# GpSimd makes the reciprocal roots of a supergroup ahead of its row numbers

## What is computed

```python
# attention: adj is (4096, 4096)
Wh = layernorm(x) @ W_w + W_b
e = leaky_relu((Wh @ a1)[:, None] + (Wh @ a2)[None, :], 0.2)
x = x + softmax(where(adj > 0, e, NEG), axis=1) @ Wh
# mixture of experts on the layernorm of the new x
z = layernorm(x)
score = z @ Wg.T + bg
top, which = top_k(score, 2); share = softmax(top)
x = x + sum over the two of share * (relu(z @ W1[e].T + b1[e]) @ W2[e].T + b2[e])
```

## Times and profile before

| | |
|---|---|
| time, median of 3 runs | 423.79 us (420.24 to 423.88) |
| span of the profiled execution | 449.1 us |
| mean granted TensorE clock in it | 0.967 of full |
| PE busy | 395.9 us, 88% |
| DVE busy | 296.4 us, 66% |
| ACT busy | 264.4 us, 59% |
| POOL busy | 202.6 us, 45% |
| POOL L770 (power) | 3 times, 5.3 us in all |
| PE L1567, the attention product | 576 matmuls, 238.9 us |

### The profile page before, as it was taken

One profiled execution on the slowest core, in us unless ns is written; L12 is line 12 of the kernel. 1 busy time (PEld: TensorE's weight loads), 2 busy tenths in 40 slices (PEclk: granted clock), 3 DMA queues, 4 the chain that ended last, 5 costly groups with the idle time before them and its releaser, 6 DMA issues.

```text
span 449.1 us, 8413 instructions
## 1 busy us (share of the span) xinstructions
PE 395.9 (88%) x2434; PEld 262.5 (58%) x2434; DVE 296.4 (66%) x816; ACT 264.4 (59%) x451; POOL 202.6 (45%) x247
## 2 busy tenths in 40 slices
PE   2699999999999999979999999897779869899970
PEld 1355555354444444434665777686669859888960
DVE  5889879988999797999877931788105731111163
ACT  1688888377687667923679544374246425555530
POOL 3473421000416742065531777756665554455460
PEclk9799999999999999998999999999989989999995
DMA  6999998879699997975869763754655545565794
GB/s 213 362 413 351 325 318 296 357 272 377 248 329 316 343 402 266 314 283 164 306 202 375 245 192 117 215 197 160 210 193 178 186 161 179 192 210 184 238 347 139
DMA packets 45612, 116.46 MB, mean 259 GB/s; under 512 B 7517, under 2 KB 19682, under 8 KB 38902
## 3 DMA queue, kind: packets, MB, share of 16 engines
q1 hardware_dynamic: 37494, 100.81, 62.9%
q0 software_dynamic: 4320, 8.47, 5.7%
q10 hardware_dynamic: 3744, 6.56, 4.9%
HBM read 84.57 MB, written 13.07 MB: 217 GB/s over the span
## 4 chain that ended last, share of the span: by engine, by line
PE 65%; issue 9%; ACT 7%; DMA 6%; DVE 4%; another core or an unknown queue 4%; SPq 3%; POOL 1%; ACTq 0%; POOLq 0%; DVEq 0%
PE acc L1567 36%; PE acc L1669 11%; ACT G_all L1334 3%; PE hps L1653 3%; PE hps L1651 3%; PE hps L1652 3%; DMA adj<-adjT 3%; DVE prob L953 2%; PE yt L1669 2%; PE yt L1612 1%; PE pj L1528 1%; DMA xbuf<-xr,slot 1%; DMA ybuf<-wst,dest 1%; SPq L546 1%
## 5 line engine op out<-in xcount | busy, mean ns | idle before, releaser
L1567 PE MATMUL acc<-prob,Wh 128*128 128x512 f32 (+1 forms) x576 | 238.9, 556 | 7.3 <-DVE Wh L892 3.6
L953 DVE SCALAR_TENSOR_TENSOR prob<-s_bc,E_col,G_all 128x1024 f32<-128x1024 f32 (+2 forms) x160 | 170.6, 1095 | 31.9 <-PE acc L1567 19.8
L1567 PEld LDWEIGHTS acc<-prob,Wh 128*128 128x128 f32 x576 | 104.8, 192 | 103.7 <-issue 89.7
L1334 ACT ACTIVATE G_all<-adj 128x2048 bf16<-128x2048 int32 (+1 forms) x67 | 118.9, 1800 | 20.0 <-DVE prob L953 10.8
L804 POOL DMA_INDIRECT ybuf<-wst,dest x71 | 73.1, 1030 | 72.1 <-ACT wst L1417 48.2
L788 POOL DMA_INDIRECT xbuf<-xr,slot x64 | 71.5, 1117 | 57.7 <-DVE slot L1110 19.6
L1669 PE MATMUL acc<-wall,prob 128*128 x368 | 52.7, 286 | 5.5 <-issue 5.5
L1669 PEld LDWEIGHTS acc<-wall,prob 128*128 128x128 f32 x368 | 45.9, 194 | 6.6 <-issue 5.9
L1407 ACT ACTIVATE prob<-hps 128x512 f32<-128x512 f32 x46 | 27.9, 607 | 32.4 <-PE hps L1653 16.6
L1205 DVE COPY share<-slab 128x1 f32<-128x1 f32 x45 | 7.0, 155 | 58.8 <-DMA slab<-xbuf 39.4
L1407 ACT ACTIVATE wst<-hps 128x512 f32<-128x512 f32 x25 | 14.9, 597 | 26.0 <-remote 17.5
(11 more groups left out here) (245 smaller groups left out, 551.6 us busy)
## 6 DMA issues: line engine op xcount, KB each, us to landing
adj<-adjT SPq DMA_DIRECT2D x52, 1024.0 KB
adj<-adjT SPq DMA_DIRECT2D x16, 768.0 KB
s_bc<-wall SPq DMA_DIRECT2D x47, 256.0 KB
wlb<-wall SPq DMA_DIRECT2D x24, 256.0 KB
slab<-xbuf SPq DMA_DIRECT2D x71, 65.0 KB
adj<-ybuf SPq DMA_DIRECT2D x6, 512.0 KB
xs<-x SPq DMA_DIRECT2D x8, 256.0 KB, 10.4
wst<-wcat ACTq DMA_DIRECT2D x8, 256.0 KB, 4.1
```

Source lines behind the costliest of these rows:

```text
L953: nc.vector.scalar_tensor_tensor(prob[n % PR][:, 0:w], c_bc[:, P * AT[g]:P * AT[g] + w], E_col[:, u:u + 1], G[m % GR][:, k * w:(k + 1) * w ...
L1334: nc.scalar.activation(G[m % GR][:, 0:w], adj_sb[m % AR][:, 0:w], ACT.Relu).then_inc(s_G, 1)
L1567: last = nc.tensor.matmul(bank[:, 0:k * P], Wh[:, u, :], prob[n % PR][:, b * P:(b + k) * P], start=(u == 0), stop=(u == TILES - 1), skip_g ...
```

## The change

In the queue of GpSimd, `row_index(g)` moves for g = 0, 1 and 2 from part 7 to part 10, and is written behind `pow_rows(g)`, which stays at part 8. Supergroups 3 and 4 keep their order. All other engines have the same instructions in the same order.

```diff
                     for g, p in parts_of(n):
                         if p == 0 and g == 0:
                             row_ends()
-                        if p == (7 if calm(g) else 9):
-                            row_index(g)
                         if calm(g) and p == 8:
                             pow_rows(g)
+                        if p == (10 if calm(g) else 9):
+                            row_index(g)
                         if not calm(g) and (p == 5 or p == 6):
                             pow_half(g, p - 5)
```

## The result

| | before | changed |
|---|---|---|
| median of 22 runs each, in turn on one chip | 423.0 us (418.8 to 426.7) | 419.8 us (415.7 to 421.9) |
| ratio, 95% interval | | 0.9947 (0.9922 to 0.9972) |
| span of the profiled execution | 449.1 us | 419.2 us |

What follows compares the result with a forecast made beforehand. PE was taken to bound the kernel (busy 395.9 of 449.1 us). A 1.12 us shorter stop plus 1.58 us of half clock avoided gave 2.7 us, from 423.8 to 421.1 us, range 419.0 to 424.8.

Steps and rivals of the forecast that it cites:

- The path: Supergroup 1: GpSimd's wait on supergroup 0's last scatter leads through power, ACT and DVE to PE's 2.55 us stop at 201.57.
- first term: Supergroup 1: power starts 1.12 us earlier (0.9 to 1.4), passed on in full, shrinking PE's stop from 2.55 to 1.43 us.
- Supergroups 0 and 2 bring nothing: GpSimd at supergroups 0 and 2: the power waits for DVE's variance, not for scatters, so nothing is gained.
- Second term: Behind PE's stop near 200 us: the shorter stop keeps the clock up, saving 1.58 us lost at half clock.
- The sum: Whole kernel: 1.12 + 1.58 = 2.7 us less, 421.1 us, 0.6% faster; chance 0.45.
- No effect: Rival for supergroup 1: scatters may land before the variance, or ACT waits for its `adj` chunk; 423.8 us, chance 0.15.
- the rival of the stop alone: PE's stop near 200 us: clock falls anyway, leaving only the 1.1 us term; 422.7 us, chance 0.20.
- The masks and the ring: Supergroup 1: ACT's `adj` chunk is there; `prob` ring place frees at 174.53, before DVE's 174.96, so DVE gains 1.12 us.
- The slower rival: First slab stays at 228.19, PE stops there 2.7 us and the clock falls; 425.4 us, chance 0.07.
- The rival of more than the sum: Two later clock falls, at 334 and 365, up to 1.7 us each, both vanish; 417.7 us, chance 0.13.

Runs made afterwards that it cites:

- supergroups 0 and 2 alone: Against the kernel before, row numbers moved behind the power for supergroups 0 and 2 only, supergroup 1 in old order; ratio 1.0028, median 423.2 us.
- late tables alone: Kernel before, GpSimd order unchanged, with supergroup 1's table parts 16 and 17 on DVE moved from steps 21 and 22 to 24 and 27; ratio 0.9936, median 420.8 us.
- the kernel before with a second power: Kernel before with the power of supergroup 1 done twice on GpSimd; ratio 1.0003 (0.9944 to 1.0062).

## Why the prediction was right, step by step

- *The path.* Right. The wait of the row numbers on the landing, through power, product, ACT's rows, ACT's masks and DVE to PE, was the whole of the first term: the delay put back by other means brings the old stop back, and earlier scatters under the old order take away as much of it as the change does.
- *Supergroups 0 and 2 bring nothing.* Right in the traces: the power waits for the variance there in both kernels.
- *First term, 1.12 us.* The product came 1.42 us earlier with respect to the variance, 1.13 from the start of the power and 0.29 from its shorter duration, the upper end that I had kept. PE's stop came to 1.39 us where I had written 1.43, and PE went on 1.40 us earlier; the difference to 2.55 - 1.39 = 1.16 is a small delay at the rank product, 0.24 us, that had no row of its own. The term was still too small for the kernel's usual course. In the five profiles with the old order and the old scatters the row numbers started 0.97, 1.28, 1.60, 1.72 and 1.97 us behind the variance, 1.5 on average, and the profile that I had was the lowest of them. The prediction took one execution's wait for the kernel's.
- *Second term, 1.58 us for the clock.* Right for stops of 1.4 us, and right in its price: 1.5 to 1.7 us by the first slab. Wrong as a fixed sum: the fall happened behind three of five stops of 2.5 to 2.6 us. As an estimate its mean is 0.6 x 1.58 = 1.0 us. This is the term that was mis-sized upward, and it offset the first.
- *The sum.* In those five profiles the power started 1.75 us behind the variance on average (1.21, 1.53, 1.85, 1.96, 2.21), and 0.08 us in the change: 1.7 us. With 1.0 for the clock that is 2.7 us; measured 2.2 us (1.2 to 3.3). The first slab says the same: in the three profiles of kernels whose supergroup 1 is that of before (before twice, supergroups 0 and 2 alone) it came 2.96, 3.19 and 1.87 us later than in the change, 2.7 on average. No effect lies well outside the measured interval, and the rival of the stop alone, 1.1 us, just below it. But the same rival with the wait at its mean, 1.7 us, lies inside: the times alone don't show the second term; what speaks for it are the profiles and the granted clock of the runs. So the forecast of 2.7 us held, with one term too small and the other too large; that the two errors cancelled is luck.
- *The masks and the ring.* Right: ACT's `adj` chunk was there, and DVE was not held by the ring; it waited 0.56 us for the masks, where the working gave 174.96 - 174.53 = 0.43.
- *The slower rival, the first slab.* It didn't happen in the change. The kernel with late tables alone stopped there for 0.93 us, so the place is as close as feared.
- *The rival of more than the sum.* The falls at 334 and 365 of the first profile are absent from the second profile of the kernel before as well. They were no part of the kernel's usual course, and 417.7 us had no ground in them.

## What to carry to other kernels

A wait in an in-order queue holds up whatever stands behind it, so put what others wait for ahead of what only you need, and compare when each becomes ready. Follow the delay along the chain to the engine that bounds the kernel: where that chain has no slack, one microsecond there is one microsecond in the end, though it may show as stops at several places, or as slow work that hides a part of them. And take more than one profile before sizing a term: here the wait ranged from 1.0 to 2.0 us from execution to execution, and the clock behind a stop came out either way.

## What the runs showed of the hardware

- A stop of PE of 2.5 to 2.6 us, with the granted clock at 1.00 ahead of it, was followed by half clock (1.2 instead of 2.4 GHz) in three profiles of five; one of 2.02 us at the rank product was too, one of 1.77 us not, and four of 1.4 us not. I had taken the fall as settled by the length.
- A fall cost 1.5 to 1.7 us where PE was what the kernel waited for, and nothing where PE still reached a stop on DVE behind it (the kernel before with a second power).
- The same power of 128x8 elements on GpSimd took 1.63 to 1.67 us in most places, but 1.96, 2.47 and 2.67 us at supergroup 1 in one profile each of three kernels, each with the same `prob` steps of DVE beside it as in kernels with 1.67, and those kept their 1.28 us. In the last of these three, late tables alone, the power of supergroup 2 was slow too, 2.37 us. The Trainium skill, GPSIMD Engine Reference, section Key points, would put contention with such DVE instructions down to shared SBUF interfaces; as they lay beside the power in all cases, these runs don't show it as the cause. It stays open.
- The last scatter of a supergroup landed 5.5 us behind its issue in the first profile, and in the kernel with late tables alone the row numbers went on 6.6 us behind the issue of that scatter (at 166.15). This is what made the wait vary from execution to execution.
